# Storing two split weights in channel order: stride-2 stationary operands instead of a chunked layout

## The chip, the cores and the metric

The kernel runs on one core of one Trainium2 chip. The metric is device time in microseconds, from runs of the whole program. The kernel before was timed three times: median 564.25 us, lowest 563.45, highest 565.81.

## The reference

One transformer-like layer on `x` of 8 x 1024 x 256, all in float32. The layer norm has no affine part; attention is linear (no softmax) and runs over 16 heads of 16 channels.

```
xn  = (x - mean(x)) / sqrt(var(x) + 1e-5)
q, k, v = split(xn @ qkv_w + qkv_b)        # 16 heads of 16
q, k = q / max(|q|, 1e-12), k / max(|k|, 1e-12)
attn = (q @ (k^T @ v) per head) @ proj_w + proj_b
ffn  = relu(xn @ W1 + b1) @ W2 + b2        # 256 -> 1024 -> 256
out  = x + attn + ffn
```

## The kernel before, in words

Every float32 matrix product is made of three fp32r matmuls: each operand is split into a high part (a rounding copy, `_hi`) and a low part (the difference, `_lo`), and `product` (line 1097) issues high by high, high by low and low by high into one PSUM bank. The left operand of `product` is the stationary one, loaded by a LDWEIGHTS ahead of every matmul; the right one is moving.

The work goes by halves of a batch: 16 halves of 512 tokens. The 1024 hidden units are taken in eight chunks `j` of 128. Per chunk, `ffn_up` (bank `w_bank`) multiplies W1 by the transposed tokens; ScalarE writes `h_hi` with a ReLU, VectorE writes `h_lo`; `ffn_down` (line 1202) adds W2 by `h` into two banks `o_bank[0]` and `o_bank[1]`, one per chunk of 128 output channels. The output channels are dealt to the two banks by parity: partition `m` of bank `k` is channel `2m + k`. So `by_chunk` (line 254) reorders columns when `w2_hi`, `w2_lo` are written (`w2_high`, ScalarE, line 604; `w2_low`, GpSimd, line 407), in four parts in the opening. Everything that reads the banks later (`yT_out`, `spread_y`) relies on that parity.

Query and key come from `query_key` (line 1147; `v_bank`): its stationary operand is a tile of `xT_hi` or `xT_lo` taken by `of_tile` (line 1106), every second column of a row of 512 floats. `gather` (line 1232; `g_bank`) has contiguous 128-column tiles as stationary operand and 256 moving columns. Once per batch, `key_value` and `project` give a 256 x 256 matrix in `g_bank`; `m_high` (ScalarE, line 590) and `m_low` (VectorE, line 914) split it into `m_hi`, `m_lo`, reordering it with `by_chunk`. `attend` (line 1268) multiplies it by the transposed queries: into `v_bank` for half 0, on top of the feed-forward sum in `o_bank` for half 1.

The last half of the last batch is the other way round: `ffn_down_last` and `attend_last` (lines 1219 and 1278) have `h` and `qT` (by `of_tile`) as stationary operands and whole rows of `w2` and `m` (`chunks`) as moving ones, 256 columns wide; the result has tokens on partitions, and `add_last` (line 942) undoes the channel order as it adds.

The order of the instructions on each engine is written by hand. TensorE's runs: `ffn_up` two chunks ahead, then `ffn_down`, and the attention products in between at fixed `j`. Batches 1 to 6 are one loop; the first, and the last, are written out.

Of the kernel before, what the change touches and what calls it, by code (L numbers as in the profile page):

```python
# [36 lines left out]
F32, F32R = mybir.dt.float32, mybir.dt.float32r  # L37
ACT = mybir.ActivationFunctionType
ALU = mybir.AluOpType
AXIS = mybir.AxisListType  # L40

P = 128
# [20 lines left out]
def build(nc, x, qkv_w, qkv_b, proj_w, proj_b, w1, b1, w2, b2, out):  # L63
# [6 lines left out]
    with ctx:  # L70
        def sb(name, shape, dtype=F32):
            return ctx.enter_context(nc.sbuf_tensor(name, shape, dtype))
# [10 lines left out]

        w1_hi, w1_lo = (sb(f"w1_{n}", [P, KC, INTER], F32R) for n in ("hi", "lo"))
        w2_hi, w2_lo = (sb(f"w2_{n}", [P, JC, KC, P], F32R) for n in ("hi", "lo"))
        wqk_hi, wqk_lo = (sb(f"wqk_{n}", [P, KC, 2 * C], F32R) for n in ("hi", "lo"))
        wv_hi, wv_lo = (sb(f"wv_{n}", [P, KC, C], F32R) for n in ("hi", "lo"))  # L90
        proj_hi, proj_lo = (sb(f"proj_{n}", [P, KC, C], F32R) for n in ("hi", "lo"))
# [23 lines left out]
        g_hi, g_lo = g_parts[:, :, 0, :], g_parts[:, :, 1, :]  # L115
        kv = sb("kv", [P, KC, P])
        kv_hi, kv_lo = (sb(f"kv_{n}", [P, KC, P], F32R) for n in ("hi", "lo"))
        m_hi, m_lo = (sb(f"m_{n}", [P, KC, KC, P], F32R) for n in ("hi", "lo"))

        ln_parts = sb("ln_parts", [P, TILES, 6])  # L120
        ln_sum, ln_dif, ln_m2, ln_mean = (sb(f"ln_{n}", [P, TILES]) for n in ("sum", "dif", "m2", "mean"))
# [128 lines left out]

        def part_columns(part):
            return (slice(None), slice(None), slice(part * 2 * P, (part + 1) * 2 * P))

        def by_chunk(columns):

            return columns.rearrange("p j (m k) -> p j k m", k=KC)

        def part_rows(part):
            return (slice(None), slice(part * 2, (part + 1) * 2))
# [122 lines left out]
        def _(pool):  # L382
# [24 lines left out]
            def w2_low(part):  # L407
                rows = part_rows(part)
                pool.wait_ge(w2_hi_ready, part + 1)
                nc.gpsimd.tensor_tensor(w2_lo[rows], by_chunk(w2_raw[rows]), w2_hi[rows].bitcast(F32),  # L410
                                        ALU.subtract).then_inc(w2_ready, 1)

            def less_first(cols):
# [77 lines left out]
        def _(act):  # L491
            def copy(to, what):
                return nc.scalar.activation(to, what, ACT.Copy)  # L493
# [95 lines left out]

            def m_high(b):  # L590
                wait(act, m_ready, b + 1)
                copy(m_hi[:], by_chunk(g_bank[:].rearrange("p (g n) -> p g n", g=KC))).then_inc(m_hi_done, 1)

            def w1_high(part):
                cols = part_columns(part)
# [8 lines left out]
            def w2_high(part):  # L604
                rows = part_rows(part)
                act.wait_ge(w2_loaded[min(part, 2)], 16)
                copy(w2_hi[rows], by_chunk(w2_raw[rows])).then_inc(w2_hi_ready, 1)

            for row, of_w1 in enumerate((b1.rearrange("(o n) -> o n", o=1), w1[0:1, :])):
                act.dma_start(raise_rows[raise_row + row:raise_row + row + 1, :], of_w1).then_inc(rows_loaded, 16)  # L610
# [124 lines left out]
        def _(dve):  # L735
            def less(to, whole, high):

                return nc.vector.tensor_tensor(to, whole, high.bitcast(F32), ALU.subtract)
# [174 lines left out]

            def m_low(b):
                wait(dve, m_hi_done, b + 1)
                less(m_lo[:], by_chunk(g_bank[:].rearrange("p (g n) -> p g n", g=KC)), m_hi[:]).then_inc(m_lo_done, 1)

            def add_attention(b, k, last):

# [22 lines left out]
            def add_last(b):  # L942

                dve.wait_ge(last_y_set, 1)
                for n, (begin, stop, bank_of) in enumerate(((0, 2, o_bank[0]), (2, 3, o_bank[1]), (3, 4, v_bank[0]))):
                    dve.wait_ge(o_ready, 2 * KC * b + KC + n + 1)
                    tiles = y_sb[:, 1, begin:stop, :].rearrange("p t (m k) -> p t m k", k=KC)
                    by_channel = bank_of[:, 0:(stop - begin) * C].rearrange("p (t k m) -> p t m k", k=KC, m=P)
                    nc.vector.tensor_tensor(tiles, by_channel, tiles, ALU.add).then_inc(last_o_done, 1)

            nc.vector.memset(warm, 0.0).then_inc(warm_set, 1)
            nc.vector.memset(raise_rows[0:raise_row], 0.0).then_inc(raise_rows_cleared, 1)
# [143 lines left out]
        def _(pe):  # L1096
            def product(to, left, right, first=True, last=True, shared=False):

                nc.tensor.matmul(to, left[0], right[0], start=first, stop=False, skip_group_check=shared)  # L1099
                nc.tensor.matmul(to, left[0], right[1], start=False, stop=False, skip_group_check=shared)  # L1100
                return nc.tensor.matmul(to, left[1], right[0], start=False, stop=last, skip_group_check=shared)  # L1101
# [93 lines left out]
                    done = part(k, 1, w1_hi, xT_lo, last=k == KC - 1)  # L1195
                done.then_inc(h_ready, 1)

            def chunks(columns):

                return columns.rearrange("p k m -> p (k m)")  # L1200

            def ffn_down(s, batch, u, j, last=False):

                if is_first(s):
                    wait(pe, w2_ready, j // 2 + 1)
                wait(pe, h_lo_done, JC * s + j + 1)
                r = j % RING
                if last and u == 1:
                    ffn_down_last(s, batch, j)
                    return  # L1210
                for k in range(KC):
                    if j == 0:
                        wait(pe, yT_copied, KC * (2 * batch + u - 1) + k + 1)
                    done = product(o_bank[k][:], (w2_hi[:, j, k, :], w2_lo[:, j, k, :]),
                                   (h_hi[:, r, :], h_lo[:, r, :]), j == 0, j == JC - 1 and u == 0, shared=True)
                    if j == JC - 1 and u == 0:
                        done.then_inc(y_ready, 1)

            def ffn_down_last(s, batch, j):

                r = j % RING
                if j == 0:
                    wait(pe, qk_copied, TILES * (s + 1))
                for t in range(TILES):
                    if j == 0 and t % 2 == 0:
                        wait(pe, yT_copied, KC * 2 * batch + 1 + t // 2)
                    apart = t == TILES - 1
                    to = v_bank[0][:, 0:C] if apart else o_bank[t // 2][:, (t % 2) * C:(t % 2 + 1) * C]
                    product(to, (of_tile(h_hi[:, r, :], t), of_tile(h_lo[:, r, :], t)),
                            (chunks(w2_hi[:, j]), chunks(w2_lo[:, j])), j == 0 and (apart or t % 2 == 0), False, shared=True)  # L1230

            def gather(s, b, u):

# [34 lines left out]
            def attend(b, u, banks):  # L1268
                wait(pe, m_lo_done, b + 1)
                wait(pe, qT_lo_done, 2 * b + u + 1)  # L1270
                for k in range(KC):
                    for g in range(KC):
                        done = product(banks[k][:], (m_hi[:, g, k, :], m_lo[:, g, k, :]),
                                       (qT_hi[:, u, g, :], qT_lo[:, u, g, :]), g == 0 and u == 0, g == KC - 1,
                                       shared=u == 1)
                    done.then_inc(o_ready, 1)

            def attend_last(b):

                wait(pe, qT_lo_done, 2 * b + 2)  # L1280
                for t in range(TILES):
                    to = v_bank[0][:, 0:C] if t == TILES - 1 else o_bank[t // 2][:, (t % 2) * C:(t % 2 + 1) * C]
                    for g in range(KC):
                        done = product(to, (of_tile(qT_hi[:, 1, g, :], t), of_tile(qT_lo[:, 1, g, :], t)),
                                       (chunks(m_hi[:, g]), chunks(m_lo[:, g])), False, g == KC - 1, shared=True)
                    if t:
                        done.then_inc(o_ready, 1)

# [99 lines left out]
```

## Time and profile before

| | |
|---|---|
| median of three runs | 564.25 us (563.45 to 565.81) |
| the profiled execution | 563.45 us, of which the span is 561.7 us |
| TensorE busy | 555.8 us (99%), 2724 matmuls, as many weight loads |
| weight loads (PEld) busy | 470.7 us (84%) |
| VectorE, ScalarE, GpSimd busy | 412.3, 282.7, 117.7 us |
| DMA | 45.36 MB, mean 81 GB/s |

PE is the matmul stream, PEld the weight loads, which the profile shows as a row of their own beside it. A matmul's row holds more than the time in which its columns stream: rows of neighbours overlap, so the distance from start to start tells the pace, not the duration. The stretch between span and execution time (1.75 us here) lies outside the instructions.

### The profile page before, as it was taken

The page shows a single profiled execution, that of the slowest core. Times are in us where ns is not written, and L with a number is a line of the kernel's source. Part 1 is how long each engine was busy: PE and PEld are TensorE (multiplying, and loading weights), DVE is VectorE, ACT ScalarE, POOL GpSimd, SP SyncE. Part 2 cuts the span into 40 slices and gives each one's busy share as a digit, 9 for nine tenths or more (in the row PEclk, how much of TensorE's full clock was granted, in tenths as well). Part 3 has the DMA queues.
Part 4 walks back from the last instruction along what each step waited for, and adds up shares of the span by engine and source line. Part 5 has one row for each costly group of instructions (what it writes and reads, how often), then busy time and mean ns, then how long its engine had stood idle before and what let it go on. Part 6 is the DMA issues. An engine that isn't in the chain of part 4 may idle for free.

```text
span 561.7 us, 8965 instructions
## 1 busy us (share of the span) xinstructions
PE 555.8 (99%) x2724; PEld 470.7 (84%) x2724; DVE 412.3 (73%) x810; ACT 282.7 (50%) x518; POOL 117.7 (21%) x148
## 2 busy tenths in 40 slices
PE   9999999999999999999999999999999999999997
PEld 7878888888888888888888888888888888888896
DVE  6797889776785867859667686876778767783745
ACT  4586474556435563374634556455553555433421
POOL 3232422402052020520214202231024201050200
PEclk9999999999999999999999999999999999999999
DMA  7422136353514545135451453425343252424423
GB/s 268 148 81 49 29 81 102 84 101 84 99 18 86 95 85 96 19 86 96 86 86 28 88 94 85 79 37 108 72 96 60 44 105 38 85 29 87 99 39 76
DMA packets 141414, 45.36 MB, mean 81 GB/s; under 512 B 133330, under 2 KB 136402, under 8 KB 141396
## 3 DMA queue, kind: packets, MB, share of 16 engines
q1 hardware_dynamic: 139280, 44.61, 39.1%
q10 hardware_dynamic: 2116, 0.53, 0.6%
q8 instruction: 9, 0.15, 0.1%
q14 instruction: 9, 0.07, 0.0%
HBM read 20.98 MB, written 8.39 MB: 52 GB/s over the span
## 4 chain that ended last, share of the span: by engine, by line
PE 97%; ACT 1%; DVE 1%; issue 0%; DVEq 0%
PE o_bank L1101 11%; PE o_bank L1099 11%; PE o_bank L1100 11%; PE w_bank L1099 10%; PE w_bank L1101 10%; PE w_bank L1100 10%; PE v_bank L1099 7%; PE v_bank L1100 6%; PE v_bank L1101 6%; PE g_bank L1099 3%; PE g_bank L1100 3%; PE g_bank L1101 3%; PE kv_bank L1254 1%; PE w_bank L1292 1%; ACT xn_first L511 0%; PE kv_bank L1256 0%
## 5 line engine op out<-in xcount | busy, mean ns | idle before, releaser
L895 DVE SCALAR_TENSOR_TENSOR h_lo<-w_bank,h_hi 128x512 fp32r<-128x512 f32 x128 | 87.4, 683 | 33.8 <-ACT h_hi L568 32.2
L568 ACT ACTIVATE h_hi<-w_bank 128x512 fp32r<-128x512 f32 x128 | 76.2, 596 | 69.8 <-PE w_bank L1101 68.7
L1099 PE MATMUL w_bank<-xT_hi,w_hi 128*128 128x512 f32 x254 | 100.3, 395 | 0.0
L1101 PE MATMUL w_bank<-xT_hi,w_lo 128*128 128x512 f32 x254 | 99.7, 393 | 0.0
L1100 PE MATMUL w_bank<-xT_lo,w_hi 128*128 128x512 f32 x254 | 99.5, 392 | 0.0
L1101 PE MATMUL o_bank<-h_hi,w_lo 128*128 128x512 f32 x240 | 94.3, 393 | 0.0
L1099 PE MATMUL o_bank<-h_hi,w_hi 128*128 128x512 f32 x240 | 93.8, 391 | 0.0
L1100 PE MATMUL o_bank<-h_lo,w_hi 128*128 128x512 f32 x240 | 93.7, 391 | 0.0
L389 POOL TENSOR_TENSOR xn_lo<-xn,xn_hi 128x256 fp32r<-128x256 f32 x56 | 41.5, 741 | 221.1 <-ACT xn_hi L493 213.7
L404 POOL TENSOR_TENSOR y_sb<-y_sb,y_rows 128x256 f32<-128x256 f32 x56 | 52.2, 938 | 129.1 <-DVE y_rows L934 106.3
L546 ACT ACTIVATE qk_sq<-v_bank 128x512 f32<-128x512 f32 x64 | 38.3, 598 | 77.4 <-PE v_bank L1101 76.9
L862 DVE TENSOR_REDUCE qk_v<-qk_sq 128x32 f32<-128x512 f32 x64 | 43.3, 679 | 35.2 <-ACT qk_sq L546 35.2
L1101 PEld LDWEIGHTS w_bank<-xT_hi,w_lo 128*128 128x128 f32 x254 | 47.7, 188 | 10.5
L1099 PEld LDWEIGHTS w_bank<-xT_hi,w_hi 128*128 128x128 f32 x254 | 47.7, 188 | 9.4 <-DVE h_lo L895 0.2
L1100 PEld LDWEIGHTS w_bank<-xT_lo,w_hi 128*128 128x128 f32 x254 | 47.7, 188 | 9.0
L1100 PEld LDWEIGHTS o_bank<-h_lo,w_hi 128*128 128x128 f32 x240 | 45.1, 188 | 10.2
L1101 PEld LDWEIGHTS o_bank<-h_hi,w_lo 128*128 128x128 f32 x240 | 45.1, 188 | 9.8
L1099 PEld LDWEIGHTS o_bank<-h_hi,w_hi 128*128 128x128 f32 x240 | 45.1, 188 | 9.7
L1099 PE MATMUL v_bank<-wqk_hi,xT_hi 128*128 128x512 f32 x128 | 50.3, 393 | 0.7 <-ACT qk_even L493 0.7
L1100 PE MATMUL v_bank<-wqk_lo,xT_hi 128*128 128x512 f32 x128 | 50.2, 392 | 0.0
L1101 PE MATMUL v_bank<-wqk_hi,xT_lo 128*128 128x512 f32 x128 | 50.0, 391 | 0.0
L511 ACT ACTIVATE xn<-x_sb,ln_offset,ln_rstd 128x256 f32<-128x256 f32 x52 | 27.0, 590 | 29.5 <-DVE ln_offset L790 29.5
(203 smaller groups left out, 984.5 us busy)
## 6 DMA issues: line engine op xcount, KB each, us to landing
qT_lo<-blocks SPq DMA_DIRECT2D x256, 32.0 KB, 1.9
x_sb<-x SPq DMA_DIRECT2D x15, 512.0 KB, 3.9
y_sb<-x SPq DMA_DIRECT2D x60, 128.0 KB, 3.4
out<-y_sb SPq DMA_DIRECT2D x58, 128.0 KB, 2.7
xT_raw<-blocks SPq DMA_DIRECT2D x224, 32.0 KB, 1.9
y_sb<-w SPq DMA_DIRECT2D x4, 256.0 KB, 4.6
x_sb<-x SPq DMA_DIRECT2D x2, 256.0 KB, 3.0
w_raw<-w SPq DMA_DIRECT2D x2, 256.0 KB, 6.8
```

Of the source, the lines that this page charges most:

```text
L389: nc.gpsimd.tensor_tensor(xn_lo[:, u, t, :], xn_of(s)[:, t, :], xn_hi[:, u, t, :].bitcast(F32), ALU.subtract).then_inc(xn_split_done, 1)
L404: nc.gpsimd.tensor_tensor(y_sb[:, u, t, :], y_sb[:, u, t, :], y_rows[:, u, t, :], ALU.add).then_inc(y_done, 1)
L511: done = nc.scalar.activation(to[:, t, :], x_sb[:, u, t, :], ACT.Identity, bias=ln_offset[:, t:t + 1], scale=ln_rstd[:, t:t + 1])
L546: nc.scalar.activation(qk_sq[:, t % 2, :], v_bank[t % 2][:], ACT.Square).then_inc(qk_sq_done, 1)
L568: nc.scalar.activation(h_hi[:, j % RING, :], w_bank[j % 2][:], ACT.Relu).then_inc(h_done, 1)
L862: nc.vector.tensor_reduce(qk_v[:, t, :], qk_sq[:, t % 2, :].rearrange("p (h d) -> p h d", d=D), AXIS.X, ALU.add).then_inc(qk_ss_done, 1)
L895: nc.vector.scalar_tensor_tensor(h_lo[:, r, :], w_bank[j % 2][:], 0.0, h_hi[:, r, :].bitcast(F32), ALU.max, ALU.subtract).then_inc(h_lo_do ...
L1099: nc.tensor.matmul(to, left[0], right[0], start=first, stop=False, skip_group_check=shared)
L1100: nc.tensor.matmul(to, left[0], right[1], start=False, stop=False, skip_group_check=shared)
L1101: return nc.tensor.matmul(to, left[1], right[0], start=False, stop=last, skip_group_check=shared)
L1254: nc.tensor.matmul(kv_raw[:, g, :, :], wv_hi[:, k, heads], g_parts[:, k, :, heads], start=g == 0 and k == 0, stop=False, skip_group_check= ...
L1292: nc.tensor.matmul(w_bank[0][:, 0:P], warm, warm, start=True, stop=True)
```

## The change

`w2_hi`, `w2_lo`, `m_hi` and `m_lo` keep their columns in channel order. The reordering `by_chunk` is gone; the two chunks are picked where the arrays are the stationary operand, by a slice with a step of 2. As moving operands (last half) they are whole rows, as before, now in channel order, and the last addition reads its banks in order. No instruction is added or removed; the sizes in memory are the same.

```diff
-        w2_hi, w2_lo = (sb(f"w2_{n}", [P, JC, KC, P], F32R) for n in ("hi", "lo"))
+        w2_hi, w2_lo = (sb(f"w2_{n}", [P, JC, C], F32R) for n in ("hi", "lo"))
-        m_hi, m_lo = (sb(f"m_{n}", [P, KC, KC, P], F32R) for n in ("hi", "lo"))
+        m_hi, m_lo = (sb(f"m_{n}", [P, KC, C], F32R) for n in ("hi", "lo"))
-        def by_chunk(columns):
-
-            return columns.rearrange("p j (m k) -> p j k m", k=KC)
...
-                nc.gpsimd.tensor_tensor(w2_lo[rows], by_chunk(w2_raw[rows]), w2_hi[rows].bitcast(F32),
+                nc.gpsimd.tensor_tensor(w2_lo[rows], w2_raw[rows], w2_hi[rows].bitcast(F32),
...
-                copy(m_hi[:], by_chunk(g_bank[:].rearrange("p (g n) -> p g n", g=KC))).then_inc(m_hi_done, 1)
+                copy(m_hi[:], g_bank[:].rearrange("p (k n) -> p k n", k=KC)).then_inc(m_hi_done, 1)
...
-                copy(w2_hi[rows], by_chunk(w2_raw[rows])).then_inc(w2_hi_ready, 1)
+                copy(w2_hi[rows], w2_raw[rows]).then_inc(w2_hi_ready, 1)
...
-                less(m_lo[:], by_chunk(g_bank[:].rearrange("p (g n) -> p g n", g=KC)), m_hi[:]).then_inc(m_lo_done, 1)
+                less(m_lo[:], g_bank[:].rearrange("p (k n) -> p k n", k=KC), m_hi[:]).then_inc(m_lo_done, 1)
...
-                    tiles = y_sb[:, 1, begin:stop, :].rearrange("p t (m k) -> p t m k", k=KC)
-                    by_channel = bank_of[:, 0:(stop - begin) * C].rearrange("p (t k m) -> p t m k", k=KC, m=P)
-                    nc.vector.tensor_tensor(tiles, by_channel, tiles, ALU.add).then_inc(last_o_done, 1)
+                    tiles = y_sb[:, 1, begin:stop, :].rearrange("p t c -> p (t c)")
+                    nc.vector.tensor_tensor(tiles, bank_of[:, 0:(stop - begin) * C], tiles, ALU.add).then_inc(last_o_done, 1)
...
-            def chunks(columns):
-
-                return columns.rearrange("p k m -> p (k m)")
+            def channels(chunk):
+
+                return slice(chunk, C, KC)
...
-                    done = product(o_bank[k][:], (w2_hi[:, j, k, :], w2_lo[:, j, k, :]),
+                    done = product(o_bank[k][:], (w2_hi[:, j, channels(k)], w2_lo[:, j, channels(k)]),
...
-                            (chunks(w2_hi[:, j]), chunks(w2_lo[:, j])), j == 0 and (apart or t % 2 == 0), False, shared=True)
+                            (w2_hi[:, j, :], w2_lo[:, j, :]), j == 0 and (apart or t % 2 == 0), False, shared=True)
...
-                        done = product(banks[k][:], (m_hi[:, g, k, :], m_lo[:, g, k, :]),
+                        done = product(banks[k][:], (m_hi[:, g, channels(k)], m_lo[:, g, channels(k)]),
...
-                                       (chunks(m_hi[:, g]), chunks(m_lo[:, g])), False, g == KC - 1, shared=True)
+                                       (m_hi[:, g, :], m_lo[:, g, :]), False, g == KC - 1, shared=True)
```

## Rows read from the trace of the kernel before

**Rows 1.** The page: engines busy; TensorE clock granted, in tenths, in 40 slices.
```profile
PE 555.8 (99%) x2724; PEld 470.7 (84%) x2724; DVE 412.3 (73%) x810; ACT 282.7 (50%) x518; POOL 117.7 (21%) x148
...
PEclk9999999999999999999999999999999999999999
```

**Rows 2.** By stretches: length, each engine's busy us (count), clock, DMA share, GB/s.
```profile
100.00:300.00 200.00, 200.00 (x961) 168.61 (x960) 148.12 (x289) 103.44 (x189) 41.87 (x50) 1.00 0.41 78
555.00:561.70 6.70, 2.65 (x23) 2.45 (x21) 1.50 (x3) 0.00 (x0) 0.00 (x0) 1.00 0.70 157
```

**Rows 3.** PE's waits and releasers: total us, times, longest us.
```profile
PE w_bank L1292 <- DVE xT_raw L951: 1.1, 1, 1.1
PE v_bank L1099 <- ACT qk_even L493: 0.7, 1, 0.7
```

**Rows 4.** The chain that ended last, opening: start us, length us.
```profile
26.83 1.11 ACT w_hi L493 x2
...
29.44 0.51 PE v_bank L1099
```

**Rows 5.** Weight loads by line: count | busy us, mean ns | idle.
```profile
L1099 PEld LDWEIGHTS o_bank<-h_hi,w_hi 128*128 128x128 f32 x240 | 45.1, 188 | 9.7
L1100 PEld LDWEIGHTS v_bank<-wqk_lo,xT_hi 128*128 128x128 f32 x128 | 24.9, 195 | 4.8
L1099 PEld LDWEIGHTS g_bank<-k_hi,xn_hi 128*128 128x128 f32 x128 | 24.2, 189 | 0.6
L1099 PEld LDWEIGHTS v_bank<-qT_hi,m_hi 128*128 128x128 f32 x28 | 5.3, 188 | 1.4 <-issue 0.3
L1100 PEld LDWEIGHTS o_bank<-w_lo,h_hi 128*128 128x128 f32 x24 | 4.7, 195 | 0.3
L1099 PEld LDWEIGHTS w_bank<-qT_hi,m_hi 128*128 128x128 f32 x4 | 0.8, 188 | 0.3 <-DVE h_lo L895 0.2
```

**Rows 6.** Timeline of PE, matmuls of 512 columns: start us, length us.
```profile
201.76 0.39 PE L1099 MATMUL o_bank<-h_hi,w_hi 128*128 128x512 f32 x1
...
203.14 0.39 PE L1099 MATMUL v_bank<-wqk_hi,xT_hi 128*128 128x512 f32 x1
...
204.52 0.40 PE L1099 MATMUL w_bank<-xT_hi,w_hi 128*128 128x512 f32 x1
```

**Rows 7.** The same, 256 columns: a gather, then the last half.
```profile
197.50 0.28 PE L1099 MATMUL g_bank<-k_hi,xn_hi 128*128 128x256 f32 x1
...
200.38 0.40 PE L1099 MATMUL w_bank<-xT_hi,w_hi 128*128 128x512 f32 x1
...
551.73 0.28 PE L1099 MATMUL o_bank<-w_hi,h_hi 128*128 128x256 f32 x1
...
554.62 0.28 PE L1099 MATMUL o_bank<-m_hi,qT_hi 128*128 128x256 f32 x1
```

**Rows 8.** Groups by line and shape: copies and subtractions on ACT and POOL.
```profile
L493 ACT ACTIVATE w_hi<-w_raw 128x512 fp32r<-128x512 f32 x4 | 2.6, 666 | 1.2 <-DMA w_raw<-w 1.2
L493 ACT ACTIVATE xT_hi<-xT_raw 128x512 fp32r<-128x512 f32 x28 | 16.0, 625 | 0.2 <-DMA xT_raw<-blocks 0.2
L493 ACT ACTIVATE m_hi<-g_bank 128x512 fp32r<-128x512 f32 x8 | 4.8, 596 | 9.2 <-PE g_bank L1101 9.2
L493 ACT ACTIVATE g_parts<-g_bank 128x512 fp32r<-128x512 f32 x8 | 4.7, 584 | 6.3 <-PE g_bank L1101 6.3
L410 POOL TENSOR_TENSOR w_lo<-w_raw,w_hi 128x512 fp32r<-128x512 f32 x4 | 5.2, 1313 | 12.3 <-ACT w_hi L493 12.3
L472 POOL TENSOR_TENSOR proj_lo<-wvp_raw,proj_hi 128x512 fp32r<-128x512 f32 x1 | 1.3, 1293 | 0.1
```

**Rows 9.** The same on DVE.
```profile
L738 DVE TENSOR_TENSOR m_lo<-g_bank,m_hi 128x512 fp32r<-128x512 f32 x8 | 5.5, 692 | 1.7 <-ACT m_hi L493 1.4
L738 DVE TENSOR_TENSOR g_parts<-g_bank,g_parts 128x512 fp32r<-128x512 f32 x8 | 5.5, 690 | 21.3 <-ACT g_parts L493 21.3
L949 DVE TENSOR_TENSOR y_sb<-o_bank,y_sb 128x512 f32<-128x512 f32 x1 | 0.7, 692 | 1.6 <-PE o_bank L1101 1.6
```

## The prediction

> **What bounds the kernel now.** I read the page first, then the stretches, PE's waits and the chain, and last the timeline of PE at single matmuls. The page has TensorE busy for 555.8 of 561.7 us, at the full granted clock, 2.4 GHz, in all 40 slices [rows 1]. Busy matmul rows overlap, so this alone doesn't say that TensorE is the limit; the stretch from 100 to 300 us does it together with the waits: PE has no idle time in 200 us [rows 2], and its waits in the whole span that name a releaser are two, 1.1 us before the first warming matmul and 0.7 us before the first query product at 29.4 us [rows 3]. From there on the kernel is a list of matmuls at a fixed pace until about 557 us; the last 4 us are the final addition and the stores [rows 2]. DVE, ACT and POOL have slack nearly everywhere, so a few ns on them are paid only in the opening and at the end. What the change does to the pace of the matmuls decides.
>
> **The stationary operands.** How many loads change: `ffn_down` outside the last half has 15 halves x 8 chunks x 2 banks x 3 = 720 (the load row of `o_bank<-h_hi,w_hi` has x240, and there are three such rows); `attend` in seven batches has 7 x 2 halves x 12 = 168 (six rows like the x28 one), and in the last batch 12 more (three rows of x4) [rows 5]. Together 900 of 2724 loads get a step of two floats instead of one.
>
> What such a load costs, the trace shows already, as the kernel has them: `query_key` and the last half load tiles of `xT`, `h` and `qT` by every second column, the same 128 x 128 float32 with the same step of 8 bytes. Its row is 195 ns (`v_bank<-wqk_lo,xT_hi`, and `o_bank<-w_lo,h_hi`) where a contiguous one is 188 or 189 [rows 5]. So each changed load should read 7 ns longer, 900 x 7 = 6.3 us in all, and the busy time of the loads should go from 470.7 to about 477 us.
>
> Does it reach the path? A load row is mostly latency, since contiguous loads in `gather` take 189 ns each and yet follow one another at 120 ns. The pace is what counts:
> - 512 moving columns: six matmuls with contiguous loads (`ffn_down`) start over 203.14 - 201.76 = 1.38 us, six with stride-2 loads (`query_key`) over 204.52 - 203.14 = 1.38 us [rows 6]. Both 230 ns per matmul. The rows have steps of 10 ns, so six could hide 10 / 6 = 1.7 ns each.
> - 256 moving columns, where a load has half the time to hide in: 24 matmuls of `gather` with contiguous loads take 200.38 - 197.50 = 2.88 us, 24 of the last half with stride-2 loads 554.62 - 551.73 = 2.89 us [rows 7]: 120.0 against 120.4 ns.
>
> A stride-2 load therefore turns over in at most 120 ns, and the changed ones stand in places with 230 ns: 110 ns of cover each. The cost I take is nothing. The bounds: below, nothing (a step of two has no reason to be quicker); above, 1.7 ns x 900 = 1.5 us by the rows of 512 columns, and 0.4 x 900 = 0.4 us by those of 256. If the cover were gone, the 6.3 us would be the first price. The moving operands don't change their reading anywhere: `h` and `qT` in `ffn_down` and `attend` are as before, and `w2` and `m` in the last half were whole contiguous rows and stay so.
>
> The Trainium skill ("SBUF — State Buffer", section on the port swizzle, its note on lines of 16 bytes) says that reading keeps full bandwidth as long as each line is hit at least twice. A step of two float32 hits each line exactly twice, so by it the change is free, and the next larger step would not be; the 120.4 ns above agree, and no run here shows the larger step.
>
> **The copies and subtractions.** All of them get contiguous reading instead of every second element:
> - `w2_high`, four copies on ACT: 666 ns; the contiguous copy of the same size and memories is `xT_hi<-xT_raw` with 625 [rows 8]. 41 ns less each. Two of the four lie on the chain: `ACT w_hi x2` at 26.83 us, from which the chain runs over ACT to the query product at 29.44 [rows 4]. That is 2 x 41 = 82 ns off the path. The other two stand earlier, where matmuls carry the chain or ACT has gaps: nothing.
> - `w2_low`, four on POOL: 1313 against 1293 ns for the like of it (`proj_lo`) [rows 8]: 20 ns each, and nobody on the chain waits for them.
> - `m_high` and `m_low`, eight each: 596 against 584 ns (`g_parts` on ACT), 692 against 690 (on DVE) [rows 8, 9]. PE reaches `attend` without an idle row after 29.4 us, so a gain of 14 ns per batch has nobody waiting for it.
> - `add_last`: its first addition took 692 ns [rows 9], with strided PSUM reading; the DVE reading of 512 contiguous PSUM columns in `g_parts` took 690. Only the last, half-size one ends the chain: nothing to 2 ns.
>
> **Sum.** Against the profiled execution of 563.45 us (span 561.7 and 1.75 beside it): 0 for the loads, -0.08 in the opening, 0 elsewhere: 563.37. That execution is the quickest of the three shown; the median is 564.25, so the forecast for the median is 564.25 - 0.08 = 564.17, which I give as 564.1 us. Below about 0.5% (2.8 us) a measurement can't tell this kernel from no change, and this is far inside.
>
> **The rivals.**
> 1. Slower: the load is exposed at 512 columns. Place: `ffn_down` and `attend`. Mechanism: a matmul starts only when its load is through, and the strided reading of `w2` beside the moving stream of `h` takes longer turns than that of `xT`. It decides once a turn exceeds 230 ns; then at least the 7 ns of the row show, 900 x 7 = 6.3 us, 564.25 + 6.3 = 570.5 us. Against it: `query_key` has the same widths of both operands, the same step and the same bank-wide output, and keeps 230 ns. For it: 720 of the loads are of an array that no row shows being read with a step. 5%.
> 2. Slower: the weight loads are the measure of the engine. Their row is 84% busy and would go from 470.7 to 477.0 us; were the time to go with it, it would be 564.25 x 477.0 / 470.7 = 571.8 us. Against it: loads of 189 ns follow at 120 ns, so a busy load row isn't a full one. 3%. The Trainium skill ("Perfetto Trace Analysis", section "Identifying the Most-Contended Engine") holds that the busy share of LDWEIGHTS tells how near TensorE is to its limit, and speaks against the change so.
> 3. No change, but more of the reordering was on the path than I count: all of it is 4 x 41 + 4 x 20 + 8 x 14 + 2 = 358 ns, so 563.9 us. For it: contiguous reading is quicker in each pair; against it: PE waits for none of these after 29.4 us. 8%, and still within 0.5%.
> 4. Faster by over 0.5%: nothing in the rows offers 2.8 us, since all the reordering is 0.36 us and the pace of TensorE has no wait to give back. 3% for what I don't see.
>
> **Chances and range.** The forecast itself has 81%, rival 3 has 8%, rivals 1 and 2 together 8%, rival 4 3%. So within 0.5%: 89%; slower 8%; faster 3%. Range: down, 564.1 less the 0.36 of rival 3 less the 0.8 by which the lowest run lies under the median, 562.9, given as 563.0; up, 564.1 + 1.5 from the bound on the loads = 565.6, and the highest run of before is 565.81, so 566.0. Outside stand mainly rivals 1, 2 and 4 with 11%.
>
> **What would show it in the profile after.** The load rows of `o_bank<-h_hi,w_hi` and of `attend` at 195 instead of 188 ns; PEld busy near 477 us; six matmuls of `ffn_down` still 1.38 us apart from the next block, and PE busy without idle time from 100 to 300 us; `w_hi<-w_raw` on ACT near 625 ns and the first query product some 0.1 us earlier; PE's waits unchanged. The prediction is wrong if the pace in `ffn_down` is over 233 ns (3 ns x 900 = 2.7 us), or if a load row stands well above 195 ns, since then the step does to `w2` what it doesn't do to `xT`.

## The result: 0.5% slower

The changed kernel takes 567.6 us (median of 16 runs, 567.01 to 569.56) against 564.21 us of the kernel before measured beside it (16 runs). The ratio is 1.0053, 95% interval 1.0044 to 1.0062. The forecast was 564.1 us, 563.0 to 566.0, with 8% for slower: the time lies outside the range and on the side that it gave little chance. The profiled execution took 567.40 us, span 565.7; the one of the kernel before was its quickest, 563.45 us. So the two traces lie 4.0 us apart where the medians lie 3.4 apart.

The page of the changed kernel, part 1, answers to [rows 1]; it is followed by PE's waits [rows 3], and by the stretch from 100 to 300 us (columns as in [rows 2]):

```profile
span 565.7 us, 8965 instructions
PE 559.5 (99%) x2724; PEld 476.5 (84%) x2724; DVE 412.4 (73%) x810; ACT 282.5 (50%) x518; POOL 117.4 (21%) x148
```

```profile
PE w_bank L1286 <- DVE xT_raw L945: 1.1, 1, 1.1
PE v_bank L1093 <- ACT qk_even L488: 0.5, 1, 0.5
PE v_bank L1118 <- DMA y_sb<-w: 0.4, 1, 0.4
```

```profile
100.00:300.00 200.00, 200.00 (x957) 169.65 (x956) 147.03 (x289) 103.18 (x189) 40.64 (x50) 1.00 0.41 78
```

TensorE still has no idle time in the middle, and no wait has come in beyond 0.4 us in the opening. It only does less in the same time: 957 matmuls in 200 us where it did 961. The busy time of the loads is 476.5 us; 477 was forecast.

Groups by line of the changed kernel, answering to [rows 5] and [rows 8] (count | busy us, mean ns | idle before):

```profile
L1093 PEld LDWEIGHTS o_bank<-h_hi,w_hi 128*128 128x128 f32 x240 | 46.5, 194 | 9.5
L1094 PEld LDWEIGHTS v_bank<-wqk_lo,xT_hi 128*128 128x128 f32 x128 | 24.8, 194 | 4.6
L1093 PEld LDWEIGHTS v_bank<-qT_hi,m_hi 128*128 128x128 f32 x28 | 5.4, 193 | 1.2
L1094 PEld LDWEIGHTS o_bank<-w_lo,h_hi 128*128 128x128 f32 x24 | 4.7, 195 | 0.3
L488 ACT ACTIVATE w_hi<-w_raw 128x512 fp32r<-128x512 f32 x4 | 2.4, 620 | 1.1 <-DMA w_raw<-w 1.1
L488 ACT ACTIVATE m_hi<-g_bank 128x512 fp32r<-128x512 f32 x8 | 4.8, 596 | 9.3 <-PE g_bank L1095 9.3
```

The loads with a step take 194 to 195 ns (193 in `attend`), `w2_high` is at 620 ns. Row by row the changed instructions do what was forecast. The pace does not. Timeline of PE in the changed kernel (start us, length us), `ffn_down` as in [rows 6], and twelve matmuls of `attend` in `o_bank`:

```profile
203.02 0.39 PE L1093 MATMUL o_bank<-h_hi,w_hi 128*128 128x512 f32 x1
...
204.42 0.39 PE L1093 MATMUL v_bank<-wqk_hi,xT_hi 128*128 128x512 f32 x1
...
224.12 0.39 PE L1093 MATMUL o_bank<-qT_hi,m_hi 128*128 128x512 f32 x1
...
226.93 0.40 PE L1093 MATMUL w_bank<-xT_hi,w_hi 128*128 128x512 f32 x1
```

and the same twelve of `attend` in the kernel before, which the prediction did not look at:

```profile
222.65 0.39 PE L1099 MATMUL o_bank<-qT_hi,m_hi 128*128 128x512 f32 x1
...
225.37 0.39 PE L1099 MATMUL w_bank<-xT_hi,w_hi 128*128 128x512 f32 x1
```

Six matmuls of `ffn_down` take 204.42 - 203.02 = 1.40 us instead of 1.38, twelve of `attend` 226.93 - 224.12 = 2.81 us instead of 225.37 - 222.65 = 2.72. The rows have steps of 10 ns; the starts in the traces, which go by 1 ns, give 233.3 ns each in this stretch of `attend` instead of 226.7.

To see where the 4.0 us of span went, I summed the distances from each matmul's start to the next over both whole traces, the first 130 matmuls (to about 30 us) together and the rest by kind:

| | before, us | after, us | difference |
|---|---|---|---|
| `ffn_down`, 512 columns, x696 | 159.52 | 161.94 | +2.42 |
| `attend`, x168 | 38.32 | 39.18 | +0.86 |
| `query_key`, x370 | 84.99 | 85.13 | +0.14 |
| `ffn_up`, x732 | 168.59 | 168.83 | +0.24 |
| `gather`, 256 columns, x384 | 46.02 | 45.95 | -0.07 |
| the first 130 matmuls | 28.89 | 29.25 | +0.36 |

3.3 of the 4.0 us lie in the 864 matmuls counted here whose loads have a step now (per matmul 3.5 ns in `ffn_down`, 5.1 in `attend`), 0.4 in their neighbours `query_key` and `ffn_up`, and 0.4 in the opening. The opening's share is hardly the change's: it holds the 0.4 us wait for the load of w1 shown above, three runs below with the copies of the kernel before have 29.37 to 29.43 us there as well, and it makes up most of the 0.6 us by which the traces differ more than the medians. So the question is why a step costs here and seemed to cost nothing in `query_key` [rows 6].

### The profile page after: what moved, and what is told of

Read it like the earlier page. It is cut to its first block, busy times and chain, and to the rows that moved or that the text cites. A ratio compares the mean times of both kernels' runs of the same rounds, so it can differ in the third digit from the quotient of the medians.

```text
span 565.7 us, 8965 instructions
## 1 busy us (share of the span) xinstructions
PE 559.5 (99%) x2724; PEld 476.5 (84%) x2724; DVE 412.4 (73%) x810; ACT 282.5 (50%) x518; POOL 117.4 (21%) x148
## 4 chain that ended last, share of the span: by engine, by line
PE 96%; ACT 1%; DVE 1%; DMA 1%; SPq 0%; issue 0%; DVEq 0%
PE o_bank L1093 11%; PE o_bank L1094 11%; PE o_bank L1095 11%; PE w_bank L1093 10%; PE w_bank L1095 10%; PE w_bank L1094 10%; PE v_bank L1093 6%; PE v_bank L1094 6%; PE v_bank L1095 6%; PE g_bank L1095 3%; PE g_bank L1094 3%; PE g_bank L1093 3%; PE kv_bank L1248 1%; DMA y_sb<-w 1%; ACT xn_first L506 0%; PE kv_bank L1250 0%
## 5 line engine op out<-in xcount | busy, mean ns | idle before, releaser
L1094 PEld LDWEIGHTS o_bank<-h_lo,w_hi 128*128 128x128 f32 x240 | 46.9, 195 | 9.4
L1093 PEld LDWEIGHTS o_bank<-h_hi,w_hi 128*128 128x128 f32 x240 | 46.5, 194 | 9.5
L1095 PEld LDWEIGHTS o_bank<-h_hi,w_lo 128*128 128x128 f32 x240 | 46.7, 195 | 9.2
```

## The experiments

**The change for one array at a time.** First w2 with channel order and m in chunks; in the last half m is then a moving operand read in permuted order. (Against the changed kernel, and cut: the split of m and its use in `attend` go back to chunks as well.)

```diff
-        m_hi, m_lo = (sb(f"m_{n}", [P, KC, C], F32R) for n in ("hi", "lo"))
+        m_hi, m_lo = (sb(f"m_{n}", [P, KC, KC, P], F32R) for n in ("hi", "lo"))
...
-                                       (m_hi[:, g, :], m_lo[:, g, :]), False, g == KC - 1, shared=True)
+                                       (in_order(m_hi[:, g]), in_order(m_lo[:, g])), False, g == KC - 1, shared=True)
```

> The change for w2 alone: 720 loads with a step of two, m as before (in the last half m is read as a moving operand with a permuted order, so that the sums stay right: 24 matmuls of 256 columns). After the change the trace has ffn_down at 232.6 ns per matmul where it had 229.2. Theory A (the pace of a 512-column matmul whose load has a step of two is longer by a few ns, load by load): 720 x 3.4 = 2.4 us more than before, so ratio 1.0043. Theory B (the loss is one of attend, or of both arrays together, and ffn_down only shows a shifted phase): under 1 us, ratio below 1.002.

Measured: 566.64 us, ratio 1.0043 (1.0031 to 1.0055). `ffn_down` in its timeline:

```profile
207.01 0.39 PE L1097 MATMUL o_bank<-h_hi,w_hi 128*128 128x512 f32 x1
...
208.41 0.39 PE L1097 MATMUL v_bank<-wqk_hi,xT_hi 128*128 128x512 f32 x1
```

1.40 us for six, and 161.99 us for the 696 in all; `attend` is back at 38.17 us. Theory A holds for w2.

Then m alone, w2 in chunks; in the last half m is read by chunks out of whole rows, a moving operand with a step of two. (Again against the changed kernel, and cut.)

```diff
-                    done = product(o_bank[k][:], (w2_hi[:, j, channels(k)], w2_lo[:, j, channels(k)]),
+                    done = product(o_bank[k][:], (w2_hi[:, j, k, :], w2_lo[:, j, k, :]),
...
-                                       (m_hi[:, g, :], m_lo[:, g, :]), False, g == KC - 1, shared=True)
+                                       (by_chunks(m_hi[:, g]), by_chunks(m_lo[:, g])), False, g == KC - 1, shared=True)
```

> The change for m alone: 180 loads with a step of two, w2 as before (in the last half m is read as a moving operand in the chunked order). Theory A: attend went from 226.4 and 229.8 ns to 233.3, so 84 x 7.0 + 84 x 3.3 + some for the last 12 = 0.9 us, ratio 1.0016. Theory B, where attend is the place of the loss: 2 us or more, ratio from 1.0035.

Measured: 566.18 us, ratio 1.0036 (1.0024 to 1.0048), which looks like theory B. It is not: `attend` grew by 0.88 us as theory A has it, and the rest comes from my own detour. The matmuls of the last half that read m with a step as moving operand:

```profile
555.60 0.39 PE L1099 MATMUL o_bank<-m_hi,qT_hi 128*128 128x256 f32 x1
...
559.72 0.41 PE L1099 MATMUL v_bank<-m_hi,qT_hi 128*128 128x256 f32 x1
```

(559.72 - 555.60) / 18 = 229 ns each where the kernel before has 120, 2.5 us over the 23 distances between them; the execution then ends 1.3 us sooner after the last matmul (3.1 us behind its start for 4.4; why is left open). Without that detour m's share is the 0.9 us.

**The step taken away where the kernel before already had one.**

```diff
-                               (of_tile(xT_hi[:, u, k, :], t), of_tile(xT_lo[:, u, k, :], t)),
+                               (xT_hi[:, u, k, tile(t)], xT_lo[:, u, k, tile(t)]),
```

> The kernel before, with the 384 stationary operands of query_key read as contiguous columns instead of every second one (queries and keys are then those of tokens in another order, so this run's output is not the reference's; the instructions are the same). Theory A, where every load with a step pays: query_key stands at 229.7 ns per matmul and falls by 1 to 3.3 ns, 0.4 to 1.3 us less, ratio 0.9977 to 0.9993. Theory B (what costs is w2's and m's place in memory, not the step): no change, ratio 1.000, and query_key stays at 229.7.

Measured: 565.8 us, ratio 1.0025 (1.0014 to 1.0035): slower, and neither theory had that. `query_key` in its timeline:

```profile
205.82 0.39 PE L1099 MATMUL v_bank<-wqk_hi,xT_hi 128*128 128x512 f32 x1
...
207.22 0.39 PE L1099 MATMUL w_bank<-xT_hi,w_hi 128*128 128x512 f32 x1
```

1.40 us for six contiguous loads, against 1.38 with the step [rows 6]. Over the same 370 matmuls 86.31 us instead of 84.99, 233.3 ns each for 229.7: that is 1.3 of the 1.5 us between the medians. (The profiled execution of this kernel took 2.3 us longer in its opening besides, 1.7 of them a wait for the load of w1, which the medians don't show.) So here a step of two is the quicker one. Theory A has the wrong sign and theory B expected no change: both fall.

**Matmuls by themselves.** A kernel of its own with one stationary and one moving array, each matmul with its own load (shortened here). This one and the two that follow were executed once each.

```
still, moving = sb("still", [P, 8 * C], F32R), sb("moving", [P, 8 * C], F32R)
def step2(i): return still[:, (i // 2 % 8) * 2 * P + i % 2:(i // 2 % 8 + 1) * 2 * P:2]
for n, (of, columns) in enumerate(alone + beside):
    for i in range(COUNT):
        nc.tensor.matmul(banks[n % 8][:, 0:columns], of(i), moving[:, (i % 4) * 512:(i % 4) * 512 + columns], start=True, stop=True)
```

> A kernel of its own, computing only matmuls from one input block: 17 stretches of 72 matmuls, each with its own load, 128 rows, stationary operand from one array. Order: 512 columns contiguous twice, step 2, step 4; 384 columns contiguous, step 2; 256 columns contiguous, step 2, step 4; 128 columns contiguous, step 2, step 4; then 512 columns with six contiguous and six step-2 loads in turn, with one and one in turn, with contiguous loads from an odd column; last contiguous and step 2 while ACT and DVE copy and subtract beside them. Theory A: step 2 at 512 columns is slower than contiguous by 3 to 7 ns per matmul (226.7 against 233.3 as in attend), in turns about half of that. Theory B (place): both are equal, since they read the same array. At 128 columns the turn of a load itself shows: if a load with step 2 takes about as long as a contiguous one, the paces are within 10 ns; step 4 should be much slower where the reading is the limit.

Each row of the timeline here is a run of matmuls taken together (start, length, count); the pace is the length, less the last matmul's own row, over the count less one. In pairs: 512 columns contiguous, step 2; 384; 256, and there step 4 as well; 128.

```profile
29.79 11.49 PE L100 MATMUL bank<-moving,still 128*128 128x512 f32 x50
45.74 11.59 PE L100 MATMUL bank<-moving,still 128*128 128x512 f32 x49
...
77.82 9.35 PE L100 MATMUL bank<-moving,still 128*128 128x384 f32 x53
90.82 9.35 PE L100 MATMUL bank<-moving,still 128*128 128x384 f32 x53
...
102.83 6.40 PE L100 MATMUL bank<-moving,still 128*128 128x256 f32 x52
111.83 6.40 PE L100 MATMUL bank<-moving,still 128*128 128x256 f32 x52
120.76 13.46 PE L100 MATMUL bank<-moving,still 128*128 128x256 f32 x57
...
136.75 6.42 PE L100 MATMUL bank<-moving,still 128*128 128x128 f32 x56
144.75 6.52 PE L100 MATMUL bank<-moving,still 128*128 128x128 f32 x54
```

With 512 columns the last matmul's row is 0.39 us: (11.49 - 0.39) / 49 = 226.5 ns contiguous, (11.59 - 0.39) / 48 = 233.3 with step 2. From the exact starts it is 226.7 and 233.3, the same figures as in `attend`. With 384 and 256 columns both are equal, 173.3 and 120.0 ns. With 128 columns the turn of a load shows: 111.7 and 117.9 ns. Step 4 at 256 columns takes 233.3. Copies on ACT and DVE beside the matmuls changed nothing (226.7 and 233.3 again). Theory A holds against B. Six contiguous and six stepped loads in turn ran at 230.7 ns, one and one at 230.1, about the middle, as expected (the granted clock was at half for 17 us, up to about the tenth matmul of the first of these two; the 51 distances taken come after that). So the load's length isn't what the matmul waits for: it turns over in 118 ns and has at least 226.7. By the rows too the load ahead of a matmul of 512 columns ends before the matmul starts, by 36 ns on the mean when contiguous and by 38 with step 2. And yet the pace moves by 6.7 ns at 512 columns, and at the same places not at 384 or 256.

One stretch did not fit: contiguous loads that begin one column off, with the same load row of 188 ns, ran at 232.4 ns. That gave theory P, the place of the two operands to each other.

> Again only matmuls: 17 stretches of 72 matmuls with 512 moving columns, now with the two operands shifted against each other (columns of 4 bytes; stationary shift / moving shift): contiguous 0/0 twice, 0/4, 0/8, 0/16, 0/32, 16/0, 16/16, 8/0, 32/0; step 2 with 0/0, 0/16, 16/0, 16/16, 0/8, 8/0, 0/4. The reason: in the first of these kernels contiguous took 226.7 ns and step 2 took 233.3 at the same places for both operands, while in the kernel before contiguous loads take 226.7 in attend (both arrays start at 64 bytes past a multiple of 128), 229 to 231 in ffn_up and ffn_down (64 bytes apart), and 233.3 in query_key with contiguous loads. Theory P (the pace depends on how the places of the two operands stand to each other, and the step is one such influence): shifts by 16 columns against each other change the pace of contiguous loads by 2 to 7 ns, 16/16 is 226.7 like 0/0. Theory S (only the step and the waits between products matter): all contiguous stretches 226.7, all of step 2 233.3.

Measured, mean of the last 51 distances of each stretch, in ns. A place is written as the shift of the stationary operand / that of the moving one, in columns of 4 bytes:

| place | 0/0 | 0/4 | 0/8 | 0/16 | 0/32 | 8/0 | 16/0 | 16/16 | 32/0 |
|---|---|---|---|---|---|---|---|---|---|
| contiguous | 226.7 | 231.6 | 233.3 | 228.9 | 232.4 | 233.4 | 233.3 | 226.7 | 233.4 |
| step 2 | 233.3 | 233.3 | 233.3 | 233.3 | not run | 232.2 | 230.0 | 233.3 | not run |

Theory P holds, and the table has the kernel's own figures in it. What counts is how the operands stand to each other: 16/16 is as 0/0. The kernels' own column below is the mean over the trace, without the first 130 matmuls and the last 12 of `attend`. In the kernel before h and xT start 64 bytes above w2, w1 and wqk (modulo 512), m and qT stand alike:

| | place | table, ns | in the kernels, ns |
|---|---|---|---|
| `ffn_down` before | contiguous 0/16 | 228.9 | 229.2 |
| `ffn_down` after | step 2 0/16 | 233.3 | 232.7 |
| `attend` before, after | 0/0 | 226.7, 233.3 | 228.1, 233.2 (into `o_bank` 226.6, 233.3) |
| `query_key`, step 2 | 16/0 | 230.0 | 229.7 |
| `query_key`, contiguous | 16/0 | 233.3 | 233.3 |

**The scan.** The list of stretches in the kernel just before is replaced:

```diff
+        stretches = [(of, 0, 8 * n) for of in (contiguous, step2) for n in range(16)]
```

> Only matmuls of 512 columns: 32 stretches of 60. The moving operand stands n x 32 bytes, n = 0 to 15, above the place of the stationary one (modulo 512 bytes); first 16 stretches with contiguous loads, then 16 with step 2. Theory P, from what was measured: contiguous n = 0: 226.7, n = 1: 233.3, n = 2 (w1 and xT, w2 and h in the kernel before): 228.9, n = 4: 232.4, n = 14 (stationary 64 bytes above): 233.3, n = 12: 233.4; step 2 n = 0, 1, 2: 233.3, n = 14 (query_key): 230.0, n = 15: 232.2. New places between 226.7 and 235. If only the step mattered, each half would be flat. A place at which step 2 runs at 226.7 to 228 would make the change free there.

Timeline rows as above, of contiguous n = 0, 1, 2, 4, 6, 8 and of step 2 n = 0, 2, 4, 6, 14:

```profile
12.36 10.14 PE L77 MATMUL bank<-moving,still 128*128 128x512 f32 x44
...
26.05 10.43 PE L77 MATMUL bank<-moving,still 128*128 128x512 f32 x44
...
40.00 10.46 PE L77 MATMUL bank<-moving,still 128*128 128x512 f32 x45
...
67.81 10.66 PE L77 MATMUL bank<-moving,still 128*128 128x512 f32 x45
...
95.86 10.43 PE L77 MATMUL bank<-moving,still 128*128 128x512 f32 x44
...
123.79 10.36 PE L77 MATMUL bank<-moving,still 128*128 128x512 f32 x45
...
235.28 10.66 PE L77 MATMUL bank<-moving,still 128*128 128x512 f32 x45
...
263.29 10.66 PE L77 MATMUL bank<-moving,still 128*128 128x512 f32 x45
...
291.26 10.34 PE L77 MATMUL bank<-moving,still 128*128 128x512 f32 x44
...
319.11 10.28 PE L77 MATMUL bank<-moving,still 128*128 128x512 f32 x44
...
430.72 10.28 PE L77 MATMUL bank<-moving,still 128*128 128x512 f32 x44
```

With the last row of 0.39 us taken off, n = 0 is (10.14 - 0.39) / 43 = 226.7 ns, step 2 at n = 6 (10.28 - 0.39) / 43 = 230.0. Theory P holds again: neither half is flat. It repeats every 256 bytes: n = 8 is n = 0, n = 14 is n = 6. Contiguous: 226.7 at n = 0, 228.9 at n = 2, elsewhere 233.3 to 234.3. Step 2: 230.0 at n = 6, 231.4 at n = 4, 232.0 at n = 7, elsewhere 233.3. No place brings step 2 to 228. (Contiguous n = 4 had 232.4 in the kernel before this one, 233.3 here, with the operands at the same places; what ran ahead of it was another stretch.) Between the quickest and the slowest contiguous stretches the load row stays at 188 ns; what grows, by the rows, is the time between its end and the start of its matmul, from 36 to 43 ns.

**The places in the kernels.** Only unused columns of padding are added; the instructions stay the same. In the first kernel they are 16 and 112 columns; the second padding brings everything behind it back to its place modulo 512 bytes.

```diff
+        sb("padding_w1", [P, 16])
         w1_hi, w1_lo = (sb(f"w1_{n}", [P, KC, INTER], F32R) for n in ("hi", "lo"))
...
+        sb("padding_wqk", [P, 112])
         wqk_hi, wqk_lo = (sb(f"wqk_{n}", [P, KC, 2 * C], F32R) for n in ("hi", "lo"))
```

> The kernel before with two unused columns of padding in memory and nothing else: w1 and w2 now start at the same residue of 512 bytes (192) as xT and h; wqk stays 64 below xT, m and qT stay alike. Theory P (the pace of 512-column matmuls follows from the relative places of the operands, by the table of the second kernel of matmuls: contiguous 0/0 226.7, 0/16 228.9, 16/0 233.3; step 2 0/0 233.3, 16/0 230.0): ffn_up from 230.3 to 226.7 (732 matmuls, -2.6 us), ffn_down from 229.2 to 226.7 (696, -1.7 us), query_key stays: 4.3 us less, ratio 0.992. Theory S (the step alone costs, the rest is waits between products): ratio 1.000.

Measured: 562.28 us, ratio 0.9970 (0.9961 to 0.9980): faster than both kernels, by less than a half of what was expected. `ffn_down`:

```profile
205.89 0.39 PE L1101 MATMUL o_bank<-h_hi,w_hi 128*128 128x512 f32 x1
...
207.25 0.39 PE L1101 MATMUL v_bank<-wqk_hi,xT_hi 128*128 128x512 f32 x1
```

`ffn_down` takes 1.36 us for six, 227.2 ns on the mean over the trace, as expected; `ffn_up` only comes down from 230.3 to 229.6. The miss sorts by what ran ahead: the 174 matmuls of `ffn_up` behind `ffn_down` fall from 228.9 to 226.7 ns, both figures of the table, but the 312 behind `query_key` only from 229.9 to 229.6, and the 96 behind `gather` rise from 230.3 to 231.3. One such stretch behind a `gather` near 200 us has 234, 236, 228, 232, 231, 227 ns and then 227 in `ffn_down`: there it took some matmuls to fall into the quick pace. The expectation had taken the mean of all for a settled pace.

The step's cost by place, with the changed kernel:

```diff
+        sb("padding_w2", [P, 32])
         w2_hi, w2_lo = (sb(f"w2_{n}", [P, JC, C], F32R) for n in ("hi", "lo"))
...
+        sb("padding_m", [P, 16])
         m_hi, m_lo = (sb(f"m_{n}", [P, KC, C], F32R) for n in ("hi", "lo"))
```

(and 96 columns ahead of wqk, which keep the arrays behind at their residues)

> The changed kernel with padding alone: w2 starts 64 bytes above h, m 64 above qT (residues 256 and 192 of 512), the place that query_key's operands have; w1, wqk, xT as before. Theory P: ffn_down from 232.6 to 230.0 (696 matmuls, -1.8 us), attend from 233.3 to 230.0 (168, -0.55 us): about 2.3 us under the changed kernel, so 1.6 us over the kernel before, ratio 1.003. Theory S: as the changed kernel, ratio 1.0053.

Measured: 565.95 us, ratio 1.0032 (1.0019 to 1.0045), as expected of theory P. `ffn_down`:

```profile
206.82 0.39 PE L1096 MATMUL o_bank<-h_hi,w_hi 128*128 128x512 f32 x1
...
208.21 0.39 PE L1096 MATMUL v_bank<-wqk_hi,xT_hi 128*128 128x512 f32 x1
```

1.39 us for six; over the trace 231.0 ns for 232.7, and `attend` 230.4 for 233.2.

Both paddings together (16 columns ahead of w1, 16 ahead of w2, 96 ahead of wqk, 16 ahead of m):

> The changed kernel with both: w1 at xT's residue, w2 and m 64 above h and qT. Theory P: ffn_up 226.7 (-2.6 us), ffn_down and attend 230.0 (-2.3 us): 4.0 - 4.9 = 0.9 us below the kernel before, ratio 0.998, although it has the steps of two. Theory S: ratio 1.0053.

Measured: 566.62 us, ratio 1.0043 (1.0030 to 1.0056). A miss. `ffn_down` has its 230.2 ns, but `ffn_up` is at 231.5 and `attend`, at the same place as in the run before, at 233.4 instead of 230.4. The trace has both paces of `attend` in it: twelve matmuls into `o_bank` in the first batch, then the same twelve two batches later, with the same operands at the same addresses:

```profile
88.69 0.39 PE L1097 MATMUL o_bank<-qT_hi,m_hi 128*128 128x512 f32 x1
...
91.45 0.40 PE L1097 MATMUL w_bank<-xT_hi,w_hi 128*128 128x512 f32 x1
...
225.28 0.40 PE L1097 MATMUL o_bank<-qT_hi,m_hi 128*128 128x512 f32 x1
...
228.09 0.39 PE L1097 MATMUL w_bank<-xT_hi,w_hi 128*128 128x512 f32 x1
```

They take 2.76 us, 230 ns each, and 2.81 us, 234 ns; all batches from the second to the seventh have the longer time. So step and place are not all. That the way in which a stretch is entered chooses its pace is a guess that fits this and `ffn_up` above; no run tests it by itself.

A shift that should hurt:

```diff
+        sb("padding", [P, 16])
         ident = sb("ident", [P, P])
```

> The kernel before with 64 bytes of padding ahead of ident, so xT and h (and all behind them) stand 128 bytes above the residue of w1 and w2 instead of 64. Theory P, by the table (contiguous 0/32: 232.4): ffn_up from 230.3 to 232.4 (732, +1.5 us), ffn_down from 229.2 to 232.4 (696, +2.2 us), query_key to a place that the table does not have (step 2 at 32/0): between -0 and +1.3 us; together 3.7 to 5 us more, ratio 1.0066 to 1.009, as much as the change itself from a shift of 64 bytes. Theory S: ratio 1.000.

Measured: 567.14 us, ratio 1.0052 (1.0038 to 1.0066): the direction of theory P, 3.1 us where 3.7 to 5 were expected. The matmuls have the whole of it: from the start of the first to that of the last they take 5.0 us more than before (561.25 for 556.24), and the trace ends 1.2 us sooner behind the last. `query_key` came to 231.3 ns, where the scan has 231.4 for its new place. `ffn_up` in its timeline:

```profile
206.31 0.40 PE L1100 MATMUL w_bank<-xT_hi,w_hi 128*128 128x512 f32 x1
...
207.70 0.40 PE L1100 MATMUL o_bank<-h_hi,w_hi 128*128 128x512 f32 x1
```

64 bytes of nothing cost the kernel before as much as the whole change, with contiguous loads and no instruction altered: over the trace `ffn_up` 232.8 ns for 230.3, `ffn_down` 232.4 for 229.2.

Last, every array at n = 0, with `query_key`'s step and without it:

```diff
+        sb("padding_w1", [P, 16])
         w1_hi, w1_lo = (sb(f"w1_{n}", [P, KC, INTER], F32R) for n in ("hi", "lo"))
...
+        sb("padding_wv", [P, 112])
         wv_hi, wv_lo = (sb(f"wv_{n}", [P, KC, C], F32R) for n in ("hi", "lo"))
```

> The kernel before with padding alone: w1, w2 and wqk all at the residue of xT and h (n = 0 of the scan). query_key keeps its step of two, now at n = 0. Theory P: ffn_down at 226.7; query_key from 229.7 to 233.3 (370 matmuls, +1.3 us against before_placed's 230); ffn_up 226.7 to 230 as in before_placed. Against before_placed +1.0 us, against the kernel before 0 to -0.5: ratio 0.999.

> The same padding, and query_key's stationary operands read as contiguous columns (queries and keys are those of tokens in another order, so the output is not the reference's; the instructions are the same). Every 512-column matmul is then contiguous at n = 0. Theory P: all at 226.7, 2.4 + 1.7 + 1.1 = 5.2 us or so less than the kernel before, ratio 0.991, with ffn_up no longer disturbed by what runs ahead of it. The two kernels of this call differ in the step of 384 loads alone: 370 x 6.7 = 2.5 us and what the neighbours lose. Had contiguous loads in query_key a price of their own, as in qk_contig (233.3), it would show here again.

Measured: 562.45 us, ratio 0.9972 (0.9963 to 0.9980), and 560.28 us, ratio 0.9931 (0.9917 to 0.9945). `ffn_down` and `query_key` with the step:

```profile
205.97 0.39 PE L1101 MATMUL o_bank<-h_hi,w_hi 128*128 128x512 f32 x1
...
207.33 0.39 PE L1101 MATMUL v_bank<-wqk_hi,xT_hi 128*128 128x512 f32 x1
...
208.73 0.28 PE L1256 MATMUL kv_bank<-g_parts,wv_hi 128*128 128x256 f32 x1
```

and without it:

```profile
205.21 0.39 PE L1101 MATMUL o_bank<-h_hi,w_hi 128*128 128x512 f32 x1
...
206.57 0.39 PE L1101 MATMUL v_bank<-wqk_hi,xT_hi 128*128 128x512 f32 x1
...
207.93 0.28 PE L1256 MATMUL kv_bank<-g_parts,wv_hi 128*128 128x256 f32 x1
```

Six of `query_key` take 1.40 us with the step and 1.36 without. Over the traces that is 86.29 and 84.12 us, 2.2 us, and the medians differ by 2.2 us. The expectation had the sign of both right; for the first it gave 0.999, too high, since `ffn_up` came down to 228.7 ns, and for the second 0.991, too low, since `ffn_up` did not reach 226.7. At a place where contiguous loads run at their best, a step of two costs 5.9 ns per matmul (2.17 us over 370). That `query_key` without the step has 227.4 ns here and had 233.3 at the place of the kernel before, with the same instructions, is the clearest pair for theory P in a whole kernel.

## Why the prediction was wrong

- What bounds the kernel: right. TensorE's list of matmuls has no idle time before or after, so what counts is the pace.
- The count of 900 loads, their 7 ns and the busy time of the loads: right (193 to 195 ns, 476.5 us).
- "The cost I take is nothing": this step failed. It was argued in two halves. That a load turns over within 120 ns is right (117.9 ns measured). That it therefore has 110 ns of cover and can't touch the pace is wrong: with 512 columns the pace takes one of several values between 226.7 and 234.3 ns, by step and place, although the load turns over in half that time and its row ends 33 to 43 ns before the matmul starts.
- The bound of 1.5 us above came from comparing `ffn_down` with `query_key`, 1.38 us each. They differ in two things, the step and the place of the operands (n = 2 and n = 14), and the two cancelled: at n = 14 contiguous loads would run at 233.3, so the step gained 3.3 ns there, while at n = 2 it costs 4.5. (The bound below, that a step has no reason to be quicker, falls with it.) The comparison of 256 columns was sound and said nothing for 512, since there the pace is 120.0 for either. A single pair was held for the effect of the step alone.
- The sum in hindsight: 696 x 3.5 = 2.4 us in `ffn_down` for 0, 168 x 5.1 = 0.9 us in `attend` for 0, 0.4 us in the neighbours for 0, and 0.4 us in the opening for -0.1, against the measured 4.0 us of span. Without the opening's wait it is some 3.6 us, against 3.4 between the medians.
- Rival 1 had the sign and the place, not the mechanism: it asked for a load turn of over 230 ns. Its 6.3 us are the 7 ns of each row laid on the path, which is nearly right for `attend` into `o_bank` by chance of its place (6.7 ns) and not elsewhere. Rival 2 falls: in the kernel with 64 bytes of padding the loads' busy time is 471.5 us, and the time is that of the changed kernel. The Trainium skill ("Perfetto Trace Analysis", section "Identifying the Most-Contended Engine") takes the busy share of LDWEIGHTS as a measure of how near TensorE is to its limit; here 471.5 and 476.5 us of it go with the same time, and the measurement decides.
- The rule of 16-byte lines in the Trainium skill ("SBUF — State Buffer", section on the port swizzle) has step 2 at full bandwidth, and by it step 4 would not be. The runs agree, nearly, for the reading itself (117.9 and 111.7 ns at 128 columns; 233.3 for step 4 at 256), yet full bandwidth of a load was not the same as no cost.
- The copies: `w2_high` went from 666 to 620 ns as forecast (625), and `m_high` stayed at 596, where 584 was forecast. (`w2_low` came to 1290 ns for a forecast of 1293, `m_low` stayed at 692.) From the start of the last two `w2_high` to the first query product it is 2.64 us for 2.70, so most of the forecast 0.08 us is there. The opening was not shorter for it: 29.25 us for 28.89 over the first 130 matmuls, since the two copies started 0.4 us later, after the wait for the load of w1 that the execution before did not have.
- "What would make the prediction wrong" named a pace over 233 ns in `ffn_down`. It was 232.7, with 3.5 ns of difference, so the threshold, set from the range and not from the bound, would have let the miss pass. And the 0.5% held to be the least that a measurement can tell was too much: the interval on 16 runs each is 0.18% wide.

What stays open: why the pace goes by the places at all. That loads and moving reads meet in the memory fits the period of 256 bytes, but no run shows it. Nor is it settled why `ffn_up` needs several matmuls to reach its pace, or why `attend` took 233.4 ns in one kernel and 230.4 in another at the same places, and both paces within one trace. So the pace of a stretch in a whole kernel can't be forecast from the table alone: of the six kernels with padding one came out as expected and one missed in sign.

## What to carry to other kernels

When matmuls run back to back, compare the start-to-start distance of every kind of them, not only that of the kind that resembles the change: rows of equal shape at 226.7, 229.2 and 229.7 ns were in the trace, and their differences were as large as the effect asked for. Before a layout is judged by half a per cent, shift the arrays by 64 bytes and measure again; here such a shift alone was worth from -0.3 to +0.5%. The quick version found here is the kernel before with two paddings, 562.3 us; with wqk moved as well it is 562.5, which the intervals don't tell apart.

## What the runs showed of the hardware that was not expected

- The pace of 512-column fp32r matmuls, each with its own load, depends on where the moving operand stands above the stationary one modulo 256 bytes, once a stretch of one kind has settled: 226.7 ns at 0, 228.9 at 64, 233.3 to 234.3 at the other multiples of 32 bytes. With a step of two in the load it is 230.0 at 192 and 231.4 at 128, else mostly 233.3.
- At n = 0 the step costs nothing at 384 columns (173.3 ns for either load) or at 256 (120.0). Other places were not run by themselves at these widths.
- The same twelve matmuls at the same addresses can run at 230 and at 234 ns within one execution.
- A moving operand with a step of two halves the rate: 229 ns for 256 columns instead of 120. The permuted reading of the run on w2, which jumps 512 bytes from column to column, left its matmuls at 120 ns.
